# GpSimd's queue in the first mixture of experts: both gathers of a pair issued ahead of the pair's second scatter

## The reference

```python
cap = int(CAP_FACTOR * T / E)                         # 1.25 * 2048 / 32 = 80
idx = jnp.argsort(-score, axis=0)[:cap].T             # 80 tokens for each expert
xe = xf[idx]
up = jnp.einsum('eci,eji->ecj', xe, w_up)             # 256 -> 2 * 512
gate, upv = jnp.split(up, 2, axis=-1)
hact = jax.nn.silu(gate) * upv
ye = jnp.einsum('ecj,eoj->eco', hact, w_down)         # 512 -> 256
out = jnp.zeros((T, C), xf.dtype).at[idx.reshape(-1)].add((w[..., None] * ye).reshape(-1, C))
```

## Time and profile before

| what | value |
|---|---|
| median of 3 timed runs | 3826.64 us (3819.09, 3826.64, 3826.94) |
| profiled execution | 3808.98 us |
| span of the profiled execution | 3807.2 us, 65854 instructions |
| PE busy | 3254.3 us, 85% of the span |
| DVE, ACT, POOL busy | 64%, 52%, 39% |
| mean granted TensorE clock | 0.908 of full speed |
| stage `experts`, first weight load to last scatter's issue | 880.3 to 1164.2 us |

### The profile page before, as it was taken

How to read it: one execution, slowest core, us unless ns; L and a number is a source line. 1 busy time by engine, 2 the same in 40 slices (tenths; PEclk the granted TensorE clock), 3 DMA queues, 4 the chain that set the end, 5 groups by cost and what they waited for, 6 DMA issues and landing times. The chain is left out here.

```text
span 3807.2 us, 65854 instructions
## 1 busy us (share of the span) xinstructions
PE 3254.3 (85%) x23031; PEld 1440.8 (38%) x23031; DVE 2444.5 (64%) x4118; ACT 1976.2 (52%) x3961; POOL 1482.6 (39%) x795
## 2 busy tenths in 40 slices
PE   4999999526885899999999986599999998969998
PEld 2323332315773232232322254122222222647776
DVE  5878896563114778778788455466666672655665
ACT  2777777331112256666666744156666665523443
POOL 2000000353222231434325240377878777415553
PEclk7989998757996799999999888699999999969999
DMA  1000000286772100100000030100000000347445
GB/s 58 12 14 11 14 8 4 90 302 244 229 240 75 31 16 7 26 5 18 18 5 9 1 109 23 31 18 10 23 10 23 9 10 24 109 145 246 84 82 118
DMA packets 163212, 239.03 MB, mean 63 GB/s; under 512 B 35859, under 2 KB 132826, under 8 KB 155994
## 3 DMA queue, kind: packets, MB, share of 16 engines
q1 hardware_dynamic: 142698, 209.40, 17.4%
q0 software_dynamic: 19056, 24.88, 3.7%
q10 hardware_dynamic: 1152, 0.79, 0.1%
HBM read 136.44 MB, written 68.92 MB: 54 GB/s over the span
## 5 line engine op out<-in xcount | busy, mean ns | idle before, releaser
L1262 DVE TENSOR_REDUCE a_part_max<-a_wb 128x1 f32<-128x512 f32 x1024 | 641.5, 683 | 110.3 <-PE a_wb L1348 101.1
L1814 DVE TENSOR_REDUCE a_part_max<-a_mx 128x2 f32<-128x1024 f32 (+1 forms) x416 | 473.3, 1180 | 264.7 <-PE a_mx L1915 264.7
L1748 ACT ACTIVATE a_e<-a_sc 128x512 f32<-128x512 f32 (+1 forms) x832 | 451.3, 594 | 231.6 <-PE a_sc L1895 225.1
L748 DVE TENSOR_REDUCE xa_part_max<-xa_mx 128x2 f32<-128x802 f32 x512 | 469.7, 985 | 103.4 <-PE xa_mx L845 102.5
L1719 POOL TENSOR_TENSOR a_part_sum<-a_part_sum,a_e 128x2048 f32<-128x2048 f32 x112 | 509.0, 4545 | 53.5 <-ACT a_e L1748 43.4
L1206 ACT ACTIVATE a_e<-a_sc 128x512 f32<-128x512 f32 x640 | 349.4, 601 | 337.7 <-PE a_sc L1373 333.0
L692 ACT ACTIVATE xa_e<-xa_sc 128x512 f32<-128x512 f32 (+1 forms) x832 | 445.8, 596 | 114.1 <-PE xa_sc L832 106.3
L1348 PE MATMUL a_wb<-a_ks,a_qs 96*128 96x512 f16 x1024 | 405.3, 402 | 25.4 <-DVEq L1289 9.5
L1895 PE MATMUL a_sc<-a_qs,a_ks 97*128 97x512 f16 (+1 forms) x832 | 277.3, 397 | 15.5 <-DMA a_qs<-a_neg_max 7.0
L868 PE MATMUL xa_po<-xa_e,xa_v 128*32 128x256 f32 (+1 forms) x3328 | 274.0, 402 | 7.4 <-ACT xa_oc L735 2.6
L1151 POOL TENSOR_TENSOR a_em<-a_e,a_later 128x512 f32<-128x512 f32 x64 | 81.0, 1266 | 459.2 <-ACT a_e L1206 371.9
(11 more groups left out here) (397 smaller groups left out, 5187.9 us busy)
## 6 DMA issues: line engine op xcount, KB each, us to landing
experts_w_up<-in_we SPq DMA_DIRECT2D x32, 1024.0 KB, 6.5
wall<-expert_halves SPq DMA_DIRECT2D x18, 1088.0 KB, 9.8
experts_w_down<-in_we SPq DMA_DIRECT2D x32, 512.0 KB, 6.1
a_qs<-a_stage SPq DMA_DIRECT2D x360, 32.0 KB, 1.8
moe_xr<-sorted_rows SPq DMA_DIRECT2D x79, 136.5 KB, 2.1
a_ks<-a_stage SPq DMA_DIRECT2D x336, 32.0 KB, 1.9
choose_whole<-in_wm SPq DMA_DIRECT2D x18, 544.0 KB, 9.0
expert_halves<-choose_cut SPq DMA_DIRECT2D x18, 544.0 KB, 7.9
```

The costliest lines, as they stand in the source:

```text
L748: dve.tensor_reduce(part_max[:, 2 * h:2 * h + 2, t, c], src[:, :, :mxw], AX.X, ALU.max).then_inc(m_taken, 1)
L1262: dve.tensor_reduce(part_max[:, j, t, k:k + 1], src[:, :mxw], AX.X, ALU.max).then_inc(unit_taken, 1)
L1748: act.activation(e[:r, m % ering, j, :], src[:r, :], ACT.Exp, scale=scale).then_inc(s_taken, 1)
L1814: dve.tensor_reduce(dst, src, AX.X, ALU.max).then_inc(m_taken, 1)
```

## The change

The scatter becomes a function like the gather, and the loop goes over pairs of experts: the pair's first scatter, then both gathers for four experts later, then the second scatter. Every wait keeps its place ahead of its own DMA, and no other engine's code is changed.

```diff
-            for e in range(4):
-                gather(e)
-            for e in range(E0):
+            def scatter(e):
                 pool.wait_ge(ye_ready, e + 1)
                 if e >= 1:
 
                     pool.wait_ge(added, 16 * e)
                 pool.indirect_dma_start(a["acc"], bass.IndirectOffsetOnAxis(slots[:CAP, e:e + 1], 0), ye[e % 2][:, :], None,
                                         compute_op=ALU.add).then_inc(added, 16)
-                if e + 4 < E0:
-                    gather(e + 4)
+
+            for e in range(4):
+                gather(e)
+            for e in range(0, E0, 2):
+                scatter(e)
+                for ahead in (e + 4, e + 5):
+                    if ahead < E0:
+                        gather(ahead)
+                scatter(e + 1)
```

## The result

| | before | after |
|---|---|---|
| median of 6 timed runs, us | 3825.53 (3813.3 to 3845.8) | 3788.13 (3770.78 to 3793.55) |
| ratio, 95% interval | | 0.9895 (0.9873 to 0.9917) |
| profiled execution: span, us | 3807.2 | 3784.8 |
| pairs 1 to 14, us | 234.14 | 197.81 |

The account below looks back on a forecast made before the run. PE, busy for 85% of the span, was taken to bound the kernel. Pairs 1 to 14 fall from 234.14 to 193.6 us, and 3826.64 - 40.5 gives some 3786 us, range 3773 to 3804.

Parts of the forecast that it names:

- Which instruction decides: First experts' stage, GpSimd: the second gather's issue time, 5.12 us into pair 1 and 3.97 into pair 13, decides PE's wait.
- When it goes out: GpSimd, pairs 1 to 14: second gather directly behind the first, at 2.25 us after the pair's start instead of 5.12.
- When it lands: Second gather's rows: landing 9.1 us after the pair's start, bounds 6.9 to 9.6, so no wait on PE.
- What a late landing costs: PE before the second turn: at most 0.4 us a pair, 5.6 us in all, with no loss of clock.
- The sum of the pairs: Pairs 1 to 14: 14 x 13.77 + 0.8 us for the adapter = 193.6 us, 40.5 less than 234.14.
- The second scatter at no cost: GpSimd: second scatter issued 0.1 to 1.3 us later, with 8.9 us of cover before the next first scatter; cost nothing.
- The weights at no cost: Up-weight loads: 9.3 us of cover against 4.9 to 8.4 us to land, DMA 12.0 us a pair; cost nothing.
- The carry to the median: Whole kernel: the stage's gain of 40.5 us taken in full off the timed median of 3826.64 us, giving 3786.1.
- the partial gain: Rival, pairs 1 to 14: second gather lands 10 to 11 us after the start; gain only 22.5 us, 3804 us; chance 0.18.
- the take-over by the weights: Rival, pairs 1 to 14: up-weights land in some 10.5 us and PE waits for them; no change, 3827 us; chance 0.05.
- the chain of scatters: Rival, GpSimd: late second scatters delay the next first scatter and both gathers; 21.6 us slower, 3848 us; chance 0.03.
- The price that the Trainium skill gives: GpSimd gathers: about 2.0 us plus bytes at 436 GB/s, so rows land before PE's turn and the change gains 0.

Follow-up runs that it names:

- the adapter experiments: Two adapter tiles, loaded a pair ahead, added to four row tiles: pairs 1 to 14 from 195.77 to 189.59 us; added to the changed kernel: median 3783.7 us against 3783.19.

## Why the prediction was right, step by step

- *Which instruction decides.* The second gather's issue time. Shown from both sides: 2.26 us after the pair's start gives 194 to 198 us, 4.0 to 5.3 us gave 234.14, and with both gathers at about 5 and 6 us it is 273.02. Within the kernel before, PE waited for rows, for 1 us or more, in every pair with an issue at 4.6 us or later, and hardly in those with one at 4.3 or earlier. The landing has its part in it: pairs 4 and 10 had the same 4.6 us, their gathers took 5.8 and 6.3 us to land, PE waited 1.04 and 1.72 us, and pair 10 alone lost the clock.
- *When it goes out.* 2.25 us was worked out; the rows have 2.27 in pair 1.
- *When it lands.* 9.1 us with bounds of 6.9 and 9.6 was taken. The tile view of the changed kernel has 4.8 to 8.0 us from issue to landing, median 6.2, where the rows before had 4.6 to 7.3:

```profile
DMA to landing us min/median/max: 4.8/6.2/8.0
```

  So the late bound is 2.26 + 8.0 = 10.2 us, 0.6 later than stated, reached in pairs 7 and 11; in the median the second gather landed after 8.3 us, earlier than was taken.
- *What a late landing costs.* This step failed at its far end. It put the wait at no more than 0.4 us, and held it to be safe for the clock because 1.47 us had been. Pair 11 stood still for 16.46 - 15.39 = 1.07 us, less than the 1.47 us of pair 5 before, and ran the next matmuls slowly:

```profile
1074.07 0.38 PE L2639 MATMUL experts_tp<-ident,experts_xe 80*128 80x80 f32 x2 [1.07 <-DVE experts_h L2708]
1074.26 3.58 PE L2665 MATMUL experts_y<-experts_w_down,experts_h 128*80 128x256 f32 x8
...
1078.11 1.89 PE L2665 MATMUL experts_y<-experts_w_down,experts_h 128*80 128x256 f32 x8
```

  The same eight of the pair's other product, 3.85 us later, took 1.89 us. That pair alone is 3.0 us over the best one. Why pair 11 lost the clock and pair 5 before did not stays open.
- *The sum of the pairs.* 193.6 us was worked out, 197.81, 194.43 and 193.91 were measured: the mean is 1.8 us higher. Two terms were too small, both of idle time, which was put at 0.8 us and was 4.6, 3.4 and 2.7 us. The adapter's waits, left at 0.8 us, were 1.6, 2.6 and 1.6; the rows' waits, put at nothing, were 2.8, 0.7 and 0.8. For the busy time 192.8 us was worked out and 193.18, 191.08 and 191.26 measured, and that fit is partly luck. The 13.77 us a pair were meant for pairs that do not wait, but pairs 2, 4 and 5 behind them had all stood still, if only for 0.06 us in pair 2, and a pair with a pause is busy longer, as the adapter experiments show; without any pause a pair takes 13.5. The changed kernel still pauses for its adapter and its rows, so the mean came near.
- *The second scatter at no cost.* Right, but with less margin than I wrote. The 4.6 us of one first scatter were called half of the cover of 8.9 us. The tile view of `experts_ye` in the changed kernel has this from issue to landing:

```profile
DMA to landing us min/median/max: 3.1/4.2/9.0
```

  The slowest, 9.0 us, took as long as that whole cover; it fell in pair 11, where the next first scatter came 11.9 us behind it. No first scatter of a pair waited for a completion in this execution; with the second scatter a little later still, two did.
- *The weights at no cost.* Right: no wait for up- or down-weights, at a DMA share of 0.86 (0.85 or more was forecast).
- *The carry to the median.* Right: 37.4 us by the medians, 36.3 to 40.2 in the stage. The spans of the changed kernel's three profiled executions differ by up to 23.4 us (3765.2 to 3788.6), of which 17.1 lie ahead of the stage's first gather and 6.7 behind pair 14; that the timed runs differ in the same places is not shown.

Of the rivals, the partial gain and the take-over by the weights did not come; the chain of scatters is real in kernels that issue the scatters later still, not in this one. The price that the Trainium skill gives in "DMA: Bandwidth & Descriptors", section "Anatomy of one DMA — SWDGE (gpsimd) path", an estimate of 2.2 us for such a gather, is met by no gather of the changed kernel's 14 pairs, the fastest of which took 4.8 us.

## What to carry to other kernels

On an engine that issues DMAs in order, put the ones that somebody waits for ahead of the ones that nobody waits for soon, and count how long the moved ones may still be late: here the scatters had 9 us in the fastest pair, and the slowest took all of that. Price a short stand-still of PE by what the next matmuls cost at the lower clock as well as by the idle time; here the two were of like size. When one late transfer is cured, look for the next one in the same pair before giving the first more slack: two adapter tiles finished what four row tiles did not.

## What the runs showed that I had not expected

- PE's clock fell after a stand-still of 1.07 us in one pair and stayed after 1.47 us in another, at the same place in the same loop. The length of the pause alone does not tell; what does is open.
- A gather of 80 rows took 4.6 to 8.0 us from issue to landing while weights streamed, and an accumulating scatter of 80 rows 3.1 to 9.0 us.
- Unchanged stages of one core moved by more than 10 us between executions: the first gather of the stage came at 878.2 to 896.4 us, with the granted clock ahead of it at 0.87 and 0.85 in the two executions compared above.
